# Context parts first in each tile, item loads moved to ScalarE's queue, destination columns stored tile by tile, in a fused attention and mixture-of-experts kernel

## The reference

```python
x = x + cross_attention(layernorm(x), ctx)      # x: 8 x 512 x 256
x = x + ffn(layernorm(x))
# cross_attention: 16 heads of 16, each query block of 64 sees only the same block of the context
scores = einsum('bhqd,bhkd->bhqk', q, k) / sqrt(16) + block_mask
out = softmax(scores) @ v ; out @ Wo + bo
# ffn: 8 experts, 1024 hidden, top 2 of the softmaxed gate, renormalized weights
h = gelu(x @ w_up[e].T) ; y = h @ w_down[e].T
out = layernorm(sum over the two chosen e of weight * y) + x
```

## Time and profile before

| | us |
|---|---|
| median of 3 runs (lowest to highest) | 857.27 (854.46 to 858.67) |
| the profiled execution: its time, its span | 856.18, 854.4 |
| busy: PE, DVE, ACT, POOL | 734.5, 541.0, 389.6, 339.0 |
| mean granted clock of TensorE | 0.935 of full speed |

### The profile page before, as it was taken

One profiled execution on the slowest core, in us unless ns is written; L12 is line 12 of the kernel. 1 busy time (PEld: TensorE's weight loads), 2 busy tenths in 40 slices (PEclk: granted clock), 3 DMA queues, 4 the chain that ended last, 5 costly groups with the idle time before them and its releaser, 6 DMA issues.

```text
span 854.4 us, 19926 instructions
## 1 busy us (share of the span) xinstructions
PE 734.5 (86%) x6340; PEld 655.7 (77%) x6340; DVE 541.0 (63%) x1292; ACT 389.6 (46%) x747; POOL 339.0 (40%) x500
## 2 busy tenths in 40 slices
PE   4788888889888888627968999999999999999990
PEld 4778887878777777416856998989988999999980
DVE  3576777786778777519425555555666667766662
ACT  3777778776667657212122222222333334433441
POOL 3344455444456455634535111111333334433453
PEclk9899999988989979858989999999999999999995
DMA  9234434333344553554673111112222233333222
GB/s 157 75 101 107 122 99 112 103 101 97 100 133 135 148 143 106 132 152 132 195 168 111 50 50 45 51 51 76 74 83 82 87 101 101 105 94 99 83 87 92
DMA packets 74090, 88.46 MB, mean 104 GB/s; under 512 B 15440, under 2 KB 64976, under 8 KB 74000
## 3 DMA queue, kind: packets, MB, share of 16 engines
q1 hardware_dynamic: 58112, 67.21, 29.2%
q0 software_dynamic: 6816, 18.65, 5.9%
q10 hardware_dynamic: 9072, 1.39, 1.8%
HBM read 53.63 MB, written 33.63 MB: 102 GB/s over the span
## 4 chain that ended last, share of the span: by engine, by line
PE 28%; issue 12%; POOL 9%; DMA 7%; SPq 2%; DVE 2%; ACT 0%; POOLq 0%; DVEq 0%
PE ps_a L589 13%; PE ps_b L605 13%; POOL y_rows L1176 4%; DMA area<-xn_rows 3%; DMA x_sorted<-area,slot_row 3%; POOL tiny L1163 2%; PE ps_c L572 1%; POOL x_sorted L1115 1%; DMA area<-x_sorted 1%; POOL tiny L1170 1%; POOL tiny L1165 1%; POOL tiny L1160 1%; DMA xn_rows<-area 1%; SPq L418 0%; SPq L419 0%
## 5 line engine op out<-in xcount | busy, mean ns | idle before, releaser
L589 PE MATMUL ps_a<-area,weights_s 128*128 128x256 f16 x1872 | 217.3, 277 | 1.9 <-DVE area L927 1.6
L605 PE MATMUL ps_b<-weights_s,area 128*128 x1872 | 210.6, 273 | 0.1
L589 PEld LDWEIGHTS ps_a<-area,weights_s 128*128 x1872 | 185.9, 100 | 26.6 <-issue 2.9
L605 PEld LDWEIGHTS ps_b<-weights_s,area 128*128 128x128 f16 x1872 | 183.1, 98 | 21.5 <-issue 0.3
L1080 ACT ACTIVATE area<-ps_a 128x512 f32<-128x512 f32 x156 | 92.6, 597 | 115.7 <-PE ps_a L589 112.7
L1176 POOL DMA_INDIRECT y_rows<-weights_s,tiny x78 | 85.9, 1101 | 127.3 <-ACT weights_s L1087 100.8
L1087 ACT ACTIVATE weights_s<-ps_b 128x512 f32<-128x512 f32 x39 | 23.3, 598 | 193.5 <-PE ps_b L605 165.6
L961 DVE SCALAR_TENSOR_TENSOR area<-area 128x512 f16<-128x512 f32 x156 | 108.0, 692 | 5.3
L1115 POOL DMA_INDIRECT x_sorted<-area,slot_row x64 | 66.2, 1034 | 54.3 <-DMA area<-xn_rows 41.2
L959 DVE TENSOR_SCALAR area<-area 128x512 f16<-128x512 f32 x156 | 66.5, 426 | 21.4 <-ACT area L1080 20.3
L1144 POOL TENSOR_TENSOR weights_s<-weights_s 128x1024 f16<-128x1024 f32 (+1 forms) x32 | 68.9, 2152 | 28.1 <-ACT weights_s L1022 27.8
(11 more groups left out here) (145 smaller groups left out, 1167.1 us busy)
## 6 DMA issues: line engine op xcount, KB each, us to landing
weights_s<-weights SPq DMA_DIRECT2D x32, 512.0 KB, 4.1
area<-x_sorted SPq DMA_DIRECT2D x39, 257.0 KB, 2.8
area<-xn_rows SPq DMA_DIRECT2D x64, 128.5 KB, 3.5
xn_rows<-area SPq DMA_DIRECT2D x32, 256.0 KB, 3.5
area<-y_rows SPq DMA_DIRECT2D x32, 256.0 KB, 2.9
resid<-x_in SPq DMA_DIRECT2D x32, 128.0 KB, 3.6
area<-ctx_t SPq DMA_DIRECT2D x32, 128.0 KB, 2.5
out<-resid SPq DMA_DIRECT2D x32, 128.0 KB, 2.8
```

The source lines that it names most:

```text
L589: mm = pe.matmul(ps_h[:, q, (ic % 2) * SLOTS:(ic % 2 + 1) * SLOTS], weights_s[:, bass.ds(first + ((2 * hc + part) * WCOLS + ic * P), P)], ...
L605: mm = pe.matmul(ps_y[:, b, v * D:(v + 1) * D], g[b][:, ic, v * P:(v + 1) * P], weights_s[:, bass.ds(first + (col + part * WCOLS), D)], st ...
```

## The change

Four edits. On ACT and on DVE the context's two parts are made earlier in the step: `ctx_hi` first of all on ACT, `ctx_lo` before the maximum of the scores (L847) on DVE. The loads of items are issued by ACT: items 0 and 1 in step 34, item 2 behind the last step, item k+4 between the second and the third Gelu of item k+1. SP, freed of them, issues all remaining row loads in one go, then the zeros. The destination column is stored with each tile by a second transfer on SP, and whoever waits for the store waits for both (32 in place of 16). The zeros have a source of their own, `pad_zero`, for which the ring gives up a slot: three slots.

```diff
-RING = 4
+RING = 3
...
+        pad_zero = carve(ROW)
...
-        pad_zero = y_s[1][:, 0:ROW]
...
 # SP, row_in
-                    if m == 0:
-                        sp.wait_ge(at_out, 16)
-                    sp.wait_ge(xn2_out[n % 2], 16 * (n // 2 + 1))
+                    sp.wait_ge(xn2_out[n % 2], 32 * (n // 2 + 1))
 # SP, step, behind the store of xn2
+                    sp.dma_start(xn_by_tile.rearrange("(c t) p d -> t p c d", c=TOPK)[bass.ds(t, 1), :, :, D:ROW].rearrange("a p c d -> p (a c) d"),
+                                 route_consts[:, R_AT:R_END].rearrange("p (c t) -> t p c", c=TOPK)[bass.ds(t, 1)].rearrange("a p c -> p (a c)").unsqueeze(2),
+                                 allow_slow_non_contiguous=True).then_inc(xn2_out[b], 16)
 # SP, behind the steps
+            for n in range(17, TILES):
+                row_in(n)
             def moe(k):
-                i = k + 4
-                if item_valid(i):
...
-                for n in {-2: (17, 18, 19, 20, 21), -1: (22, 23), 0: (24, 25, 26), 1: (27, 28, 29, 30, 31)}.get(k, ()):
-                    row_in(n)
                 if k == 0:
                     sp.wait_ge(pad_r, 2)
...
-            moe_steps(-4, moe)
+            moe_steps(0, moe)
 # DVE, step: moved from behind k_bd to the place before the maximum
+                    dve.wait_ge(ctx_hi_r, t + 1)
+                    since(dve, v_ps, t)
+                    dve.scalar_tensor_tensor(ctx_lo, ctx[b], CTX_SCALE, ctx_hi, ALU.mult, ALU.subtract).then_inc(ctx_lo_r, 1)
 # DVE
-                    since(dve, xn2_out[1 - b], 16 * (half + b))
+                    since(dve, xn2_out[1 - b], 32 * (half + b))
...
 # ACT, start
-            act.dma_start(xn_rows.rearrange("(g p) d -> p g d", p=P)[:, :, D:ROW], route_consts[:, R_AT:R_END].unsqueeze(2),
-                          allow_slow_non_contiguous=True).then_inc(at_out, 16)
+            def load_item(i):
+                b = i % 2
+                if i in ROUND_OF:
+                    r = ROUND_OF[i]
+                    act.wait_ge(items_r, r + 1)
+                    rows_scattered(act, sum(ROUNDS[r][0:2]))
+                    if r == 0:
+                        act.wait_ge(k_ps, TILES)
+                    if r == 2:
+                        act.wait_ge(padded, 16 * (E + 1))
+                since(act, gt_ps, i - 1)
+                since(act, at_r, i - 1)
+                at_x = act.value_load(item_x[0:1, i:i + 1], min_val=0, max_val=SPARE)
+                act.dma_start(xg[b], x_units[bass.ds(at_x, 1)].rearrange("a p v d -> p (a v) d")).then_inc(xgot[b], 16)
 # ACT, step: ctx_hi moved to the head of the step; behind the exponentials
+                if isinstance(j, int) and 2 * j + u == 34:
+                    load_item(0)
+                    load_item(1)
 # ACT, behind the steps
+            load_item(2)
             def moe(k):
                 i = k + 1
                 if item_valid(i):
                     for q in range(GQ):
+                        if q == 2 and item_valid(k + 4):
+                            load_item(k + 4)
                         act.wait_ge(h_ps, GQ * i + 1 + q)
...
-                    if k == 1:
-                        act.wait_ge(padded, 16 * (E + 1))
```

More of the change, by code:

```diff
@@ L304, in program @@
         rt_shifted, rt_exp, rt_mask, rt_cnt, rt_read = (sem(n) for n in ("rt_shifted", "rt_exp", "rt_mask", "rt_cnt", "rt_read"))
-        rt_pos, at_out = sem("rt_pos"), sem("at_out")
+        rt_pos = sem("rt_pos")
         rt_col, rt_row = sem("rt_col"), sem("rt_row")
@@ L391, in _ @@
             steps(sp, 0, step)
-            x_units = x_sorted.rearrange("(s v p) d -> s p v d", v=SUBS, p=P)
+            for n in range(17, TILES):
+                row_in(n)
             def moe(k):
-                i = k + 4
-                if item_valid(i):
[L399 to L411, removed]
-                for n in {-2: (17, 18, 19, 20, 21), -1: (22, 23), 0: (24, 25, 26), 1: (27, 28, 29, 30, 31)}.get(k, ()):
-                    row_in(n)
                 if k == 0:
@@ L844, in step @@
                 if valid(t):
+                    dve.wait_ge(ctx_hi_r, t + 1)
+                    since(dve, v_ps, t)
+                    dve.scalar_tensor_tensor(ctx_lo, ctx[b], CTX_SCALE, ctx_hi, ALU.mult, ALU.subtract).then_inc(ctx_lo_r, 1)
+                t, half, b = here(j, u, 0)
+                if valid(t):
                     since(dve, sub_r, t)
@@ L880, in step @@
                                                  ALU.add, ALU.mult).then_inc(k_r, 1)
-                t, half, b = here(j, u, 0)
-                if valid(t):
-                    dve.wait_ge(ctx_hi_r, t + 1)
-                    since(dve, v_ps, t)
-                    dve.scalar_tensor_tensor(ctx_lo, ctx[b], CTX_SCALE, ctx_hi, ALU.mult, ALU.subtract).then_inc(ctx_lo_r, 1)
                 t, half, b = here(j, u, -1)
@@ L946, in moe @@
                     for b in range(2):
-                        dve.wait_ge(xn2_out[b], 16 * TILES // 2)
+                        dve.wait_ge(xn2_out[b], 32 * TILES // 2)
                     dve.wait_ge(x2t_ps, TILES)
@@ L986, in _ @@
             act.dma_start(rc, route_consts[:, 0:R_AT]).then_inc(rc_in, 16)
-            act.dma_start(xn_rows.rearrange("(g p) d -> p g d", p=P)[:, :, D:ROW], route_consts[:, R_AT:R_END].unsqueeze(2),
-                          allow_slow_non_contiguous=True).then_inc(at_out, 16)
             act.wait_ge(small_in, 16)
             act.wait_ge(zeroed, 2)
+            x_units = x_sorted.rearrange("(s v p) d -> s p v d", v=SUBS, p=P)
+            def load_item(i):
[12 more added lines that the diff above has]
+                act.dma_start(xg[b], x_units[bass.ds(at_x, 1)].rearrange("a p v d -> p (a v) d")).then_inc(xgot[b], 16)
             def shifted_exp(r):
@@ L997, in step @@
             def step(j, u):
+                t, half, b = here(j, u, 0)
+                if valid(t):
+                    act.wait_ge(ctx_in[b], 16 * (half + 1))
+                    since(act, v_ps, t)
+                    act.activation(ctx_hi, ctx[b], ACT.Copy, scale=CTX_SCALE).then_inc(ctx_hi_r, 1)
                 t, half, b = here(j, u, 1)
@@ L1012, in step @@
                     act.activation(prob_t, ps_pt, ACT.Copy).then_inc(pt_r, 1)
-                t, half, b = here(j, u, 0)
-                if valid(t):
-                    act.wait_ge(ctx_in[b], 16 * (half + 1))
-                    since(act, v_ps, t)
-                    act.activation(ctx_hi, ctx[b], ACT.Copy, scale=CTX_SCALE).then_inc(ctx_hi_r, 1)
                 t, half, b = here(j, u, 0)
```

## The result

The changed kernel takes **923.96 us** (median of 4 runs, 919.73 to 929.69) where the kernel before takes 857.97 (4 runs): ratio **1.078, interval 1.070 to 1.085**, 66 us slower. The forecast was 860, its range 843 to 874: the time lies 50 us above the upper end. The profiled execution took 924.17 us; its span is 922.4 against 854.4, so 68.0 us are to be found in it.

What follows compares the result with a forecast made beforehand. TensorE was taken as the bound, full from 460 us, with waits in the attention and the stretch after. Terms -4 - 6 + 0 + 1 + 12 = +3 on the profiled 856.18 gave 859.2, hence 860 against the median; range 843 to 874.

Steps and rivals of the forecast that it cites:

- regular tiles: Attention, some 18 tiles: the wait for ctx_lo becomes a wait for the held normalization; 0, bounds -15 and +5.
- column store: Attention, SP's extra transfer per tile: 0 in the steady part, +1 for the last steps, bounds 0 and +2.
- term of the attention: Attention's share of the sum: first three tiles -4, colliding tiles -6, regular tiles 0, destination columns +1.
- The collision: Regular tiles: POOL's L1144 starts ahead of DVE's second normalization L869, which then takes 2.24 us instead of 0.41.
- Rival 1: Regular tiles: no collision, the order stays, tile 8.66 us, 15 us less, 845; chance 0.15.
- First three tiles: Attention's start, where no second row is normalized yet: shorter wait at the value product, -4, bounds -5.5 and -1.
- Tiles that collide already: Attention, 11 tiles where L517 waited for L869: 0.75 each goes, less 2; -6, bounds -8 and 0.
- Transition: From attention's end to item 5's up product: item loads on ACT and ring of three cost +12, +3 to +21.
- the two stands: Transition: TensorE stands from about 377 to 404 for 22 tiles' rows, then until 469 for zeros and item 7's load.
- rounds of three slots: Transition: scatter and load through one slot take 6.3 us a round, bounds 5.6 and 7.2.

Runs made afterwards that it cites:

- e5: The whole change, with SP's load of x issued one step (a tile) earlier: 868.31 us, ratio 1.016 to the kernel before.
- e6: The whole change, with GpSimd's split of the weights made to wait for the second normalization of the same step: 876.13 us, ratio 1.026 to the kernel before.
- e8: The kernel before with context parts first, x loaded a tile earlier and GpSimd's split after the second normalization: 810.32 us, ratio 0.948.
- e1: The kernel before with the context parts made first and nothing else: 878.51 us, ratio 1.029.
- e2: The kernel before with the destination columns stored tile by tile and nothing else: 891.67 us, ratio 1.047.
- e3: The kernel before with the item loads on ACT, the ring of three and the separate zeros, nothing else: 869.88 us, ratio 1.021.
- e10: e8 with ring of three, zeros' own source and no ACT wait before the second y copy, item loads on SP: 820.27 us, 0.964 of the kernel before.
- e11: e8 with the one big store of the routing columns moved from program start to ACT's step 16: 813.10 us, 0.956 of the kernel before.

## Why the prediction was wrong

**The step that failed** is the one on the regular tiles, 0 in the sum, and, in the same way, the one on the column store, 0 as well. Of the first: "L529 then follows directly, some 0.3 later, at 130.1 to 130.5: where it is today." It followed the held normalization into TensorE and stopped there. The normalization's other reader, SP's store of its rows, was never followed, nor what is queued behind that store: the load of x. Of the second: "In the steady part nine microseconds lie between, so 0." That looked only at the next writer of `xn2`, not at the load that the new transfer is put in front of. In place of both the runs showed a loop through SP's queue, a late load of x and a held normalization that make each other late, with tiles of 12.40 us instead of 10.33. The term of the attention was -9 (-4, -6, 0, +1); measured +58: -5.5 up to the third value product, +60 in the 29 tiles and +3.4 behind the last. What the ring makes of it is shown by e5 and e6: taking the load of x or the split out of it brings the tile from 12.40 back to 10.49 or 10.63.

**The collision itself was right.** In the kernel after one of the two normalizations is held in 27 of 32 tiles, in 23 of them the first, where the forecast had the second (before 8, the first once). The price was right too as long as x is there: the regular tiles stood at 0 in the sum and the tile of before is 10.33; e5, with the collision and x early, has 10.49. The rule of the Trainium skill, "SBUF — State Buffer", section "Who interferes with whom", which the prediction leaned on for the collision, agrees in kind: 2.33 and 2.22 instead of 0.40 where both overlap, and in e6 to e8 one single normalization is held, in the third step. Rival 1's tile without the collision, 8.66, is close to the 8.82 of e8. But the rival would not have come true from the change alone, and the run that keeps the order by a wait also needs x early: e6 has no collision and 10.63.

**First three tiles**: -4 forecast, the third value product came at 37.81 instead of 43.32, -5.5, the bound; e1 with the context parts alone has 36.78, e2 with the column store alone 43.37, so it is the context parts' doing. **Tiles that collide already**: the -6 is not to be seen, because 27 of 32 tiles became of that kind and worse; and of the 11 tiles that the forecast counted by L517's wait, 8 had a normalization held.

**Transition**: +12 forecast, +10 measured, and it was no luck: the two stands are where the text put them. The first was to last from 15 to 42 us behind the attention's end (377 and 404 against 362.2); TensorE stood from 435.1 to 461.80, that is from 14.9 to 41.7 behind 420.15. The second was to end 106.8 behind it (469); it ended 104.8 behind (524.92), and the 24 matmuls after it took 4.12 instead of 2.78. Between them item 3's load came 40.4 behind the attention's end (forecast 41.8), the last load of rows 86.6 (88.8) and item 7's load 103.4 (104.8). In e3, the load move alone, item 5's up product ends 111.3 behind the attention's end, +12.5. The reason given, rounds of three slots and zeros behind the last rows, fits what e10 shows; that the item loads stand on ACT makes no difference to the total there.

**The range** held nothing of this, because every bound was a bound on a cost that had been seen, taken once. The sum had no term for a loop through a queue, in which a late turn makes the next one late.

**TensorE's clock** followed. The stretch from 60 to 300 us, the windows of the kernel after, of the kernel before, and of e8 (start:end, length, busy of each engine, granted clock, DMA share, GB/s):

```profile
60.00:300.00 240.00, 193.10 (x1464) 173.05 (x1464) 171.50 (x398) 147.73 (x291) 90.79 (x138) 0.86 0.38 89
```

```profile
60.00:300.00 240.00, 208.34 (x1758) 187.97 (x1757) 181.96 (x479) 174.19 (x350) 114.44 (x172) 0.94 0.41 115
```

```profile
60.00:300.00 240.00, 230.36 (x2054) 209.85 (x2054) 200.13 (x561) 203.73 (x407) 139.89 (x201) 1.00 0.52 136
```

The granted clock lies at one of two levels, 1.2 and 2.4 GHz, and these are means over both. A matmul takes 193.10 / 1464 = 132 ns in the kernel after, 119 before and 112 in e8: the waits of the ring cost once as waits and once more as slow products behind them (the output product took 1.91 at 125.21, behind a wait of 2.52 and at the lower level, 1.03 in the earlier trace rows). TensorE's busy time for the same 6340 matmuls is 757.1 instead of 734.5; how much of the 60 us this is was not measured by itself.

## What to carry to other kernels

When an instruction gets later, follow every reader of its result, stores included, and then what stands behind that store in the issuing queue: a load there is late too, and if the late instruction depends on a later turn of that load, the loop sets the time and not the sum of the stalls. Before putting a transfer into a queue, look at the margin with which the load behind it lands (here 1.2 us of a tile of 9.5), and move such a load ahead of the store before anything else. And when a long instruction holds up what runs beside it, place it against all of its neighbours at once: moved away from one it held up another, neither edit alone gained here, and together they gained 5 per cent.

## What the runs showed of the hardware

**Four-byte pieces cost their neighbours.** The big store of 8192 pieces, 32 KB, takes 18 to 26 us from issue to landing over the runs; in e11 the load of 128 KB that SP issued 2.2 us behind it (160.48 against 158.24) let TensorE start at 173.11, 12.6 later, where such a load takes 2.5 in the median of the kernel before, and SP's next issue of a load of x took 1.10 instead of 0.35. The tile by tile store of 1 KB in 256 pieces takes longer to land than the 256 KB issued ahead of it. The transfers of the kernel after (KB each, median us from issue to landing):

```profile
weights_s<-weights SPq DMA_DIRECT2D x32, 512.0 KB, 5.7
...
xn_rows<-area SPq DMA_DIRECT2D x32, 256.0 KB, 4.5
...
resid<-x_in SPq DMA_DIRECT2D x32, 128.0 KB, 4.8
area<-ctx_t SPq DMA_DIRECT2D x32, 128.0 KB, 4.5
...
xn_rows<-route_consts SPq DMA_DIRECT2D x32, 1.0 KB, 5.4
```

Before, the first four take 4.1, 3.5, 3.6 and 2.5. The table of specifications in the Trainium skill, "DMA: Bandwidth & Descriptors", section "Specifications", asks for 512 bytes or more in a piece for full rate; the direction agrees, the delay of the neighbours is this case's.

**Who is held is not to be read from starts that lie close.** In the tile shown, L852 starts at 134.58, by the record 0.05 ahead of the split at 134.63, and it is L852 that is held, for 2.33. So it is in six tiles of the kernel after, 0.04 or 0.05 ahead, with 2.31 to 2.33, and in a seventh, 0.01 ahead, with 2.29; in the others that are held the split starts first and the normalization takes up to 2.27. Over all the runs the line is sharp: a normalization that starts up to 0.08 ahead of the split is held (for 2.35 at the most), one that starts 0.09 or more ahead takes its 0.4, and it is the split that gets longer, 2.31 at 0.09, 2.23 to 2.25 at 0.15 and its usual 2.13 from 0.26 on. The rule of the Trainium skill, "SBUF — State Buffer", section "Who interferes with whom", says that whichever starts first keeps the ports; by the recorded starts that holds from 0.09 us on.
